# Windowed attention block with routed experts: the softmax maximum applied as the bias of 32 small exponentials per strip, in place of four large ones and four subtractions on GpSimd

## The reference

```
xn   = layernorm of x over the 64 channels (viewed as windows of 64 tokens x 64 features)
q,k,v = xn @ Wq + bq, xn @ Wkv + bkv           # 4 heads of 16
attn = softmax(q * 16**-0.5 @ k^T + rel_bias)  # 64 x 64 per window and head
x    = x + (attn @ v) @ Wproj + bproj
t    = tokens of x, each normalised over its 64 features
x    = x + mix of the 2 best of 8 experts per token, by a softmax router
```

## Time and profile before

| what | value |
|---|---|
| median of 3 runs | 1396.92 us (1395.99 to 1397.34) |
| the profiled execution, its own time | 1397.41 us |
| its span, first to last instruction | 1395.6 us |
| mean granted TensorE clock | 0.986 |
| busy: PE, DVE, ACT, POOL | 87%, 83%, 63%, 63% of the span |

### The profile page before, as it was taken

How to read it: one execution, slowest core, us unless ns; L and a number is a source line. 1 busy time by engine, 2 the same in 40 slices (tenths; PEclk the granted TensorE clock), 3 DMA queues, 4 the chain that set the end, 5 groups by cost and what they waited for, 6 DMA issues and landing times.

```text
span 1395.6 us, 47420 instructions
## 1 busy us (share of the span) xinstructions
PE 1208.6 (87%) x19715; PEld 786.3 (56%) x19840; DVE 1161.0 (83%) x2476; ACT 877.3 (63%) x1617; POOL 880.6 (63%) x758
## 2 busy tenths in 40 slices
PE   4288999988999999988999999998899999999985
PEld 3266565555566656555555655665565555665541
DVE  7738888888888888888888888889888888888875
ACT  5356676666666667666666766765766666666642
POOL 0246776765766677685666667777666666666642
PEclk9979999999999999999999999999999999999998
DMA  6003332321222333332122323322222222222221
GB/s 176 16 11 72 86 84 67 86 64 41 57 64 67 69 86 78 73 71 60 46 56 64 85 67 85 87 64 56 57 49 64 56 65 62 50 58 57 64 63 38
DMA packets 95552, 91.52 MB, mean 66 GB/s; under 512 B 26797, under 2 KB 62253, under 8 KB 95342
## 3 DMA queue, kind: packets, MB, share of 16 engines
q1 hardware_dynamic: 95342, 88.49, 27.3%
HBM read 36.03 MB, written 17.83 MB: 39 GB/s over the span
## 4 chain that ended last, share of the span: by engine, by line
PE 45%; DVE 27%; issue 12%; ACT 10%; DMA 4%; POOL 1%; SPq 1%; DVEq 0%; POOLq 0%; ACTq 0%
PE bank_y L521 11%; DVE t_g L978 8%; PE bank_s L405 7%; PE bank_s L379 6%; DVE mx L870 5%; PE bank_o L433 5%; PE bank_p L448 4%; DVE sums L808 4%; ACT k_m L641 3%; PE bank_t L420 3%; DVE prob L863 3%; PE bank_p L510 3%; ACT g_t L689 2%; PE bank_g L510 2%; PE bank_t L389 2%
## 5 line engine op out<-in xcount | busy, mean ns | idle before, releaser
L1070 POOL TENSOR_TENSOR prob<-prob,mx 128x512 f32<-128x512 f32 x256 | 261.6, 1043 | 92.5 <-DVE mx L870 92.5
L521 PE MATMUL bank_y<-t_g,w_exp 128*64 128x512 f32 x1024 | 267.1, 616 | 18.1 <-DVE t_g L978 17.2
L1092 POOL TENSOR_TENSOR t_g<-t_t,g_copy 128x512 f32<-128x512 f32 x128 | 165.3, 1291 | 176.2 <-ACT g_copy L693 176.2
L661 ACT ACTIVATE prob<-prob 128x512 f32<-128x512 f32 x256 | 161.0, 629 | 148.1 <-POOL prob L1070 146.4
L665 ACT ACTIVATE prob_t<-bank_t 128x512 f32<-128x512 f32 x256 | 152.6, 596 | 146.3 <-PE bank_t L420 146.3
L863 DVE TENSOR_TENSOR prob<-bank_s,rel 128x1024 f32<-128x1024 f32 x128 | 156.6, 1223 | 82.1 <-PE bank_s L405 82.0
L1082 POOL TENSOR_TENSOR ln<-ln,mhalf 128x8 f32<-128x8 f32 x64 | 105.0, 1640 | 158.5 <-DVE ln L906 158.5
L420 PEld LDWEIGHTS bank_t<-idn,prob 128*128 128x128 f32 x1024 | 110.7, 144 | 146.2 <-issue 115.9
L420 PE MATMUL bank_t<-idn,prob 128*128 128x128 f32 x1024 | 168.6, 288 | 25.2 <-ACT prob_t L665 19.6
L978 DVE TENSOR_TENSOR t_g<-t_t,bank_p 128x512 f32<-128x512 f32 x256 | 173.7, 679 | 4.0 <-PE bank_p L510 3.9
L405 PEld LDWEIGHTS bank_s<-k_m,q_t 32*64 32x64 f32 x4096 | 114.6, 136 | 72.8 <-issue 69.2
(11 more groups left out here) (111 smaller groups left out, 2369.6 us busy)
## 6 DMA issues: line engine op xcount, KB each, us to landing
t_t<-t_rout SPq DMA_DIRECT2D x256, 128.0 KB, 3.7
x_in<-in_x SPq DMA_DIRECT2D x68, 256.0 KB, 3.5
r_b<-recip_rows SPq DMA_DIRECT2D x64, 256.0 KB
out_y<-y_out SPq DMA_DIRECT2D x128, 128.0 KB, 2.5
r_in<-sum_b SPq DMA_DIRECT2D x64, 16.0 KB
recip_rows<-r_out SPq DMA_DIRECT2D x64, 16.0 KB, 1.4
gate_sel<-in_sel SPq DMA_DIRECT2D x1, 512.0 KB
rel<-in_relb SPq DMA_DIRECT2D x1, 256.0 KB
```

The lines of the kernel that those rows point to most:

```text
L521: mm(B_Y[C * a:C * a + C, :], w_exp[:, pair, :], t_g[:, (2 * pair + a) % TG, :], start=False, stop=(pair == MIXES // 2 - 1), skip_group_ch ...
L661: A(prob[:, i], prob[:, i], ACT.Exp).then_inc(p_ready.sem, 1)
L1070: G.tensor_tensor(sc, sc, mx[:, i, :].unsqueeze(2).broadcast_to([P, 2 * HEADS, NTOK]), ALU.subtract).then_inc(s_shifted.sem, 1)
L1092: G.tensor_tensor(t_g[:, u % TG, :], t_t[:, p, u % 2, :], g_copy[:, n % 2, :], ALU.mult).then_inc(tg_pool.sem, 1)
```

## The change

GpSimd's `shift` and its semaphore are removed. ScalarE's `exps` now waits for VectorE's maxima itself and applies the maximum as the bias operand of the activation. A bias is one value per partition, and a unit has eight rows with a maximum each, so a unit takes eight instructions of 64 columns. Because the engine adds the bias, the stored scores are negated: q is scaled by the negative factor, rel is subtracted in place of added, the maximum becomes a minimum, and the exponential has scale -1. TensorE waits for the eighth exponential of a unit.

```diff
-        s_shifted = sem("s_shifted", UNITS)
-        p_ready = sem("p_ready", UNITS)
+        p_ready = sem("p_ready", UNITS * 2 * HEADS)
...
-                pe.wait_ge(p_ready.sem, p_ready.at(g, i + 1))
+                pe.wait_ge(p_ready.sem, p_ready.at(g, (i + 1) * 2 * HEADS))
...
-                A(q_bias[:, :], b_qkv[:, 0:1], ACT.Copy, scale=float(DH) ** -0.5).then_inc(set_act.sem, 1)
+                A(q_bias[:, :], b_qkv[:, 0:1], ACT.Copy, scale=-float(DH) ** -0.5).then_inc(set_act.sem, 1)
...
-                  ACT.Identity, bias=q_bias[:, :], scale=float(DH) ** -0.5).then_inc(q_ready.sem, 1)
+                  ACT.Identity, bias=q_bias[:, :], scale=-float(DH) ** -0.5).then_inc(q_ready.sem, 1)
...
             def exps(g, i):
-                act.wait_ge(s_shifted.sem, s_shifted.at(g, i + 1))
-                A(prob[:, i], prob[:, i], ACT.Exp).then_inc(p_ready.sem, 1)
+                act.wait_ge(mx_ready.sem, mx_ready.at(g, i // 2 + 1))
+                for h in range(HEADS):
+                    for n in range(2):
+                        at = h * 2 + n
+                        A(prob[:, i, h, n, :], prob[:, i, h, n, :], ACT.Exp, bias=mx[:, i, at:at + 1],
+                          scale=-1.0).then_inc(p_ready.sem, 1)
...
-                                    [P, 2, 2, HEADS * NTOK]), ALU.add).then_inc(s_biased.sem, 1)
+                                    [P, 2, 2, HEADS * NTOK]), ALU.subtract).then_inc(s_biased.sem, 1)
...
-                                ALU.max).then_inc(mx_ready.sem, 1)
+                                ALU.min).then_inc(mx_ready.sem, 1)
...
-            def shift(g, i):
-                pool.wait_ge(mx_ready.sem, mx_ready.at(g, i // 2 + 1))
-                sc = prob[:, i].rearrange("p h n k -> p (h n) k")
-                G.tensor_tensor(sc, sc, mx[:, i, :].unsqueeze(2).broadcast_to([P, 2 * HEADS, NTOK]),
-                                ALU.subtract).then_inc(s_shifted.sem, 1)
...
-                if attending:
-                    shift(j, 2)
-                    shift(j, 3)
...
-                if projecting:
-                    shift(j + 1, 0)
-                    shift(j + 1, 1)
```

## The result

The changed kernel takes 1477.97 us (median of 4 runs, 1476.23 to 1478.57), the kernel before 1397.13 us (4 runs, 1395.99 to 1400.48). The ratio is 1.0574, with a 95% interval of 1.0547 to 1.0602. The forecast was 1479.

A forecast was written before the change was run, and what follows sets the result against it. TensorE was busiest (87%, 45% of the chain); ScalarE and GpSimd were not taken as the bound. To 1397.4 us came 55 for 24 take slots and 26 for 37 quiet ones: 1479 us, 8 in 10 range 1430 to 1550.

The forecast's parts named there:

- The price of one small exponential: ScalarE's 64-column exponential with bias: 0.350 us start to end, 0.24 in the queue; eight add 1.40 us per unit.
- Bounds: Queue time of one small exponential: 0.14 us if the operand fetch is hidden, 0.35 if nothing overlaps.
- Nothing for GpSimd's part: Removing 256 subtractions, 261.6 us of GpSimd, was counted as no gain, since GpSimd has 1% of the chain.
- Units 2 and 3, take slot: TensorE's second take waits for copy_probs 2 and starts 2.52 us late; the slot gets 2.3 us longer.
- Units 2 and 3, quiet slot: Later copy_probs 2 delays turn_probs 3 from 705.35 to 706.05; the slot gets 0.7 us longer.
- What would make it wrong: The square's lateness adding up each slot, quiet slots growing as much as take slots; or VectorE setting the take slot.
- The sum: 24 take slots at 2.3 us (55) and 37 quiet slots at 0.7 (26) added to 1397.4: 1479 us.
- (a): Rival: small exponentials don't overlap, each holding ScalarE's queue 0.35 us; 107 us more, 1586 us; chance 0.08.
- (b): Rival: TensorE's clock falls to 0.82 in take slots, 2.1 us each, 50 us more: 1529 us; chance 0.15.
- (c): Rival: not slower; small exponentials hold ScalarE's queue at most 0.10 us each: 1397 us; chance 0.07.

The follow-up runs named there:

- e4: Changed kernel with one 512-column exponential per unit, the first row's maximum as bias for all eight rows (computation changed): 1393.34 us, ratio 0.9967.
- e1: Changed kernel with small exponentials only in units 2 and 3; units 0 and 1 keep GpSimd's subtraction and one large exponential: 1451.37 us, ratio 1.0382.
- e6: Changed kernel with copy_probs 2 ahead of unit 3's exponentials and, in take slots, the first square_planes behind copy_probs 3: 1481.94 us, ratio 1.0588.
- e2: Changed kernel with small exponentials only in units 0 and 1; GpSimd subtracts for units 2 and 3: 1425.34 us, ratio 1.0195.
- e3: Changed kernel with eight small exponentials per unit but no bias operand; GpSimd subtracts for all four units as before: 1475.11 us, ratio 1.0557.
- e7: Changed kernel with four 128-column exponentials per unit, each using one row's maximum for two rows (computation changed): 1405.62 us, ratio 1.0047.
- e9: Changed kernel with small exponentials only in unit 0; GpSimd subtracts for units 1 to 3: 1398.01 us, ratio 0.9997.
- e10: e6 with unit 1's exponentials also moved behind the square, so both queue moves on the changed kernel: 1442.05 us, ratio 1.0320.
- e12: e3 with unit 1's exponentials moved behind the square: 1411.09 us, ratio 1.0092.
- e11: e2 with unit 1's exponentials moved behind the square: 1404.32 us, ratio 1.0037.

## Why the prediction was right, and where it wasn't

The time came out 1 us from the forecast. The price of an instruction and the take slots were forecast rightly; how a quiet slot gets longer was not. Growth of the inner slots was forecast too large and of the rest too small, and that the two cancelled to within 1 us is luck.

- **The price of one small exponential**: forecast 0.350 us from start to end and 0.24 a step; measured 0.339 and 0.239. Bounds (0.14 and 0.35) weren't needed. The estimate from the Trainium skill ("ScalarE: Activation LUTs", What ACT_TABLE_LOAD costs) gave 240 ns, and the trace agrees. ScalarE was forecast at 1235 us and measured 1224.0, GpSimd at 619 and 623.6.
- **Nothing for GpSimd's part**: right to 0.3% (e4). The 146 us of waiting in the earlier trace rows were worth under 4 us to the kernel before.
- **Units 2 and 3, take slot**: forecast 2.3 us longer, measured 2.1. The mechanism, TensorE's second take behind copy_probs 2, is seen in the trace (1.37 us), and e1 shows 1.7 us from these units alone. The other 0.4 are units 0 and 1 (e1 against the changed kernel). The forecast had 0.2 for them. What it lacked is that in a take slot the way round runs through all four units; e6 showed it by failing.
- **Units 2 and 3, quiet slot**: forecast 0.7 us, measured 0.5, and this is the step that was wrong in its mechanism. Its pieces were near: from the maxima to the square 5.72 us were forecast, and the changed kernel takes 762.94 - 757.23 = 5.71; unit 2 to copy_probs 2 was to be 4.93 and is 774.62 - 769.74 = 4.88. But the prediction made one pass over the old slot and put the growth at turn_probs 3. Slots repeat, and what sets their length is the whole way round, 19.69 us through all four units. Each pair of units shares in it: units 2 and 3 alone cost 0.2 (e1), units 0 and 1 alone 0.4 (e2).
- **What would make it wrong**: the prediction named the square's lateness adding up in each slot. It does add up, by 0.4 to 0.5 us and not by the 2 us of a take slot, since about 0.3 of the 0.73 us is slack (e2, e3).
- **The sum**: 21 inner take slots grew by 44 us and 25 inner quiet slots by 12, against a forecast of 48 and 18. The 17 intervals left over (the filling, the first take slots, the turns of the images) grew by 20 us, against a forecast of 15, and the part before the first copy_sums by 3.5, against nothing.
- **Rivals**: (a) is excluded by the 0.239 us. (b) is excluded for the take slots: their granted clock is 1.00. TensorE is busy for 86% of one and not for the 82% that (b) reckoned with, since its busy time grew from 18.86 to 19.71 us for as many matmuls; why isn't shown. At the turns of the images something of (b) does show (below). (c) is excluded for the change as made; e7 and e9 show where it begins.

**TensorE's clock at the turns.** In each of the three turns from one image to the next TensorE waits 2.75 us for unit 2's exponentials, where the kernel before waits 1.13, and behind two of the three the granted clock falls. One of the two, the pause (in brackets) and the stretch behind it (columns as in the earlier trace rows):

```profile
710.82 0.66 PE L419 MATMUL bank_t<-idn,prob 128*128 128x128 f32 x4 [2.75 <-ACT prob L663]
```

```profile
711.00:714.00 3.00, 2.79 (x39) 2.05 (x40) 2.19 (x7) 3.00 (x11) 2.60 (x3) 0.69 0.00 0
```

Those two intervals grew by 2.2 and 2.0 us, the third by 1.0, so the clock has about 2 of the 81 us; this is an estimate from these three, and no run separates it. The section that the prediction cites from the Trainium skill's "TensorE: Matmul & The Clock Gate" is titled "Why this matters for your kernels"; it ties drops to pauses between bursts of matmuls. Here the pauses of 1.37 us in the take slots left the clock at 1.00, and behind the longer ones it fell twice in three times.

No version that keeps the computation was faster than the kernel before: e9 equals it, and e4, which changes the computation, is the fastest at 0.3% less. The best order that was tried with all 2048 small exponentials and their bias operand (e10) still is 3.2% slower; without the operand, and with GpSimd's subtractions kept, it is 0.9% (e12).

## What to carry to other kernels

Before paying one engine for another's work, ask what the wait that goes away was worth: here 146 us of waiting was worth under 4. It isn't slack to be spent either: where units 0 and 1 got longer and the wait stayed (e3), the slots grew with them. Price small instructions by their step in the queue, and then look for rings that lead back to the same instruction in the next round: additions on a ring cost in full beyond its slack (0.3 us on one here, 1.1 on another) and off it little (e11), and moving one queue entry off the ring (e3 to e12: 64 us) can be worth more than making all of them cheaper. A move that gains nothing may only be behind a second ring through the same work (e6, e10).

## What the runs showed of the hardware

A bias operand from memory isn't hidden behind the instruction before it: 64-column exponentials step by 0.239 us with it and 0.147 without (changed kernel, e3), and the step grows with the columns, 0.293 at 128 (e7). A single large exponential went from 0.629 to 0.720 us with the operand (e4).

TensorE's granted clock stayed at 1.00 through pauses of 1.37 us in every take slot of the changed kernel. After a pause of 2.75 us, the same in three turns of the images, it fell in two of them, to 0.93 over the interval from one copy_sums to the next, and stayed at 1.00 in the third.
